# Moving the C-row multiply of 49 scan steps from VectorE to GpSimd

## The chip, the cores and the metric

The kernel runs on one core of one Trainium2 chip. The metric is the device time of one execution in microseconds.

## What is computed

Two layers act on x of shape (4, 1024, 128) in fp32. Layer 0 adds to x the product of a Mamba block (a selective scan with 256 inner channels and 16 states) and a gated mixture of experts (8 experts, 2 chosen per token, and a shared one). Layer 1 does the same with an attention without softmax, and a second mixture of experts. The part that the change touches is the selective scan:

```python
dA = jnp.exp(dt[..., None] * A)
dBx = (dt * xc)[..., None] * Bm[:, :, None, :]
def step(h, inp):
    dA_t, dBx_t, C_t = inp
    h = dA_t * h + dBx_t
    y = jnp.einsum('bdn,bn->bd', h, C_t)
    return (h, y)
_, ys = lax.scan(step, h0, (dA, dBx, Cm))        # over time
y = (ys + xc * D_param) * silu(z)
```

## The kernel before, in words

Time is cut into eight chunks of 512, of which the last is two segments of 256. In each of the nine segments there are 16 scan steps, one for each state n, so there are 144 steps, N = 0 to 143; steps 0 to 111 are wide (512 columns in each of two halves of the channels) and 112 to 143 narrow (256). Channels lie on the partitions, time along the free axis. A segment that starts in the middle of a batch entry needs, for each state, the last column of the segment before it; that column is kept in `carry` by steps 0 to 15, 32 to 47, 64 to 79 and 96 to 127.

One step N is shared by the engines:

- ACT computes exp(dt * A) into `pA` in PSUM (line 1016, function `decay`, for step N+1 while step N is scanned). It waits for the product of step N, since `pA` is one buffer, and for the carried column, which ACT itself copies (line 1162). It then issues the DMA that loads the B and C rows of step N+3, spread over all partitions, into `bcb` (line 1025, `bc_load`), which waits until step N has let go of that buffer.
- GpSimd multiplies dt*x by the B row into `dBx` (line 805), for step N+1 as soon as the first scan of step N is over.
- VectorE does two scans in place in `pA` (line 1429) and then multiplies `pA` by the C row into `hc` in SBUF (line 1437). `hc` has two buffers; the multiply waits until the transposes of step N-2 have read the one it writes.
- TensorE transposes `hc` (line 902, `hflip`, eight transposes in a wide step, four in a narrow one) and sums the states in the PSUM tensor `pH`.

Beside the scan every step carries other work, and its order is written out by `make_plan`; all engines walk the same list and each does its own part of every item. A step is "a scan b hflip", or "a scan b c hflip" when a second job starts. The slots a, b and c are pipelined expert jobs: `gate` is two VectorE operations (lines 1465 and 1477, each with one operand in PSUM), `up` two matmuls of TensorE with a tanh on ACT (lines 1181, 1186), and `flip` transposes and the down matmuls, read back by ACT (lines 1196, 1199). Slots a and c are of lane 0, b of lane 1. Behind `hflip` come the step's extras: parts of the mixer's front (conv, line 1377; subtraction, line 1402; softplus and others), normalisation (line 1243), routing (lines 1293 to 1363), the combination of expert outputs (partly on GpSimd, lines 774 and 778), and scatters and gathers, which GpSimd issues as indirect DMAs. Many of VectorE's extras are linked: each waits for a semaphore of the one before.

Of the kernel before, what the change touches and what calls it, by code (L numbers as in the profile page):

```python
# [11 lines left out]
P = 128  # L12
# [5 lines left out]
NS = 16  # L18
# [59 lines left out]
def make_plan():  # L78
# [175 lines left out]
    plan += [("decay", 0)]  # L254
    running, waiting = [None, None], [None, None]
# [26 lines left out]
    for step in range(max(end + 3, max(extras) + 1)):  # L282
# [8 lines left out]
        for what in order:  # L291
# [4 lines left out]
            elif what == "scan":  # L296
                if ends_chunk:
                    plan.append(("accT", q - 1))
                if live:
                    plan.append(("scan", step))  # L300
            elif what in ("a", "b", "c"):
                new = starts.get((step, 0), {}).get("ab".find(what)) if what != "c" else starts[step, 1][0]
                before_slot = len(plan)
                slot(1 if what == "b" else 0, new, step)
                if what.upper() in order and (what == "b" or running[0] is None or lanes[0][running[0]][0] == 1) and len(plan) > before_slot and plan[-1][0] == "flip":
                    held.append((what, plan.pop()))
# [5 lines left out]
            elif what == "hflip":  # L312
                if ends_chunk:
                    plan.append(("y", q - 1))
                if live:
                    plan.append(("hflip", step))
                if ends_chunk:
                    plan.append(("mix_out", q - 1))
# [9 lines left out]
def program(nc, T, out):  # L328
# [29 lines left out]
    for N in range(STEPS):  # L358
        s, n = divmod(N, NS)
        if s + 1 < len(SEGS) and SEGS[s + 1][0] // 2 == SEGS[s][0] // 2:  # L360
            carry_no[N] = len(carry_no) + 1
            carry_after[N + NS] = carry_no[N]

# [11 lines left out]
    with ExitStack() as ctx:  # L375
# [188 lines left out]
        zs_ready, acc_copied = sem("zs_ready"), sem("acc_copied")  # L564
        mixed_stored, gathered, fetched, combined, mid_stored, out_stored = (
# [150 lines left out]
        def _(pool):  # L716
            for kind, *a in plan:
# [75 lines left out]
                elif kind in ("decay", "scan"):  # L793
# [11 lines left out]
                    pool.tensor_tensor(dBx[:, N % 2, :, 0:t1 - t0], dtx[q % 2][:, :, t0:t1], row, ALU.mult).then_inc(dBx_ready, 1)  # L805


        @block.tensor
        def _(pe):
# [12 lines left out]
            for kind, *a in plan:  # L822
# [68 lines left out]
                elif kind == "hflip":  # L891
# [3 lines left out]
                    pe.wait_ge(hc_ready, N + 1)  # L895
# [9 lines left out]
                elif kind == "busy":  # L905
                    pe.wait_ge(hc_ready, STEPS)
# [95 lines left out]
        def _(act):  # L1002
            A = act.activation

            def decay(N):
# [5 lines left out]
                if N:  # L1011
                    act.wait_ge(hc_ready, N)
                    if N - 1 in carry_no:
                        act.wait_ge(carried, carry_no[N - 1])
# [3 lines left out]
            def bc_load(N):  # L1018
# [3 lines left out]
                if N >= BCR:  # L1022
                    act.wait_ge(dBx_ready, N - BCR + 1)
                    act.wait_ge(hc_ready, N - BCR + 1)
                act.dma_start(*bc_row(N)).then_inc(bc_loaded[N % BCR], 16)

            for kind, *a in plan:
# [129 lines left out]
                elif kind == "scan":  # L1157
                    N, = a
                    q, t0, t1 = SEGS[N // NS]
                    if N in carry_no:  # L1160
                        act.wait_ge(hc_ready, N + 1)
# [57 lines left out]
        def _(dve):  # L1219
# [28 lines left out]
            for kind, *a in plan:  # L1248
# [172 lines left out]
                elif kind == "scan":  # L1421
# [3 lines left out]
                    if N in carry_after:  # L1425
                        dve.wait_ge(carried, carry_after[N])
                    for k in range(DK):
                        dve.wait_ge(decay_ready, 2 * N + k + 1)
                        dve.tensor_tensor_scan(pA[:, k, 0:w], pA[:, k, 0:w], dBx[:, N % 2, k, 0:w],  # L1429
                                               carry[:, k, N % NS:N % NS + 1] if N in carry_after else 0.0, ALU.mult, ALU.add  # L1430
                                               ).then_inc(h_ready, 1)

                    dve.wait_ge(h_ready, 2 * N + 2)
# [157 lines left out]
```

## Time and profile before

| what | value |
|---|---|
| time, median of 3 runs | 1128.32 us (1124.17 to 1129.85) |
| profiled execution, first to last instruction (the profile gives no other time of it) | 1123.9 us |
| VectorE busy | 960.6 us, 85% |
| TensorE busy | 895.5 us, 80% |
| GpSimd busy | 613.3 us, 55% |
| ACT busy | 607.2 us, 54% |

The profile names the engines PE (TensorE matmul), PEld (its weight load), DVE (VectorE), ACT, POOL (GpSimd) and SP. Busy time is the union of an engine's recorded instructions. A line such as L1437 is line 1437 of the kernel before. "a<-b,c" gives the written tensor and the ones read; idle time stands with what ended it.

### The profile page before, as it was taken

Reading aid. Unit: us, or ns where it says so; the run is one execution under the profiler, and the core shown is the slowest. Engines: PE = TensorE matmul, PEld = TensorE weight load, DVE = VectorE, ACT = ScalarE, POOL = GpSimd, SP = SyncE. Lnnn points to the kernel's source line nnn. Section 1 sums busy time; section 2 is a strip of 40 time slices with the busy share of each in tenths; the row PEclk is TensorE's granted clock in tenths of the full one; section 3 lists DMA queues with packets and bytes.
Section 4 is the critical chain, followed back from the end, with each engine's and each line's share of the span. In section 5 each row is a group of like instructions: output and inputs, shape, how many; then the busy total and the mean of one; then the engine's idle time right before and its main releaser. Section 6 shows DMA issues by size and latency. Waiting matters only on the chain.

```text
span 1123.9 us, 16984 instructions
## 1 busy us (share of the span) xinstructions
PE 895.5 (80%) x4556; PEld 633.1 (56%) x4556; DVE 960.6 (85%) x1804; ACT 607.2 (54%) x1593; POOL 613.3 (55%) x422
## 2 busy tenths in 40 slices
PE   3466688778787778897997799898876888889878
PEld 1344466556565555675665466665555656556556
DVE  4698878999999998998999899999969878978445
ACT  2444556574456564665666466665554555546243
POOL 1238423768634846675327855665874747425540
PEclk9986789997898898999999899999977999989999
DMA  9955344356543644565444645455742466446201
GB/s 277 298 128 133 85 101 110 119 133 180 118 101 106 141 102 117 148 164 146 111 96 127 156 129 150 102 162 145 192 111 73 109 155 159 109 102 142 73 9 34
DMA packets 168650, 144.71 MB, mean 129 GB/s; under 512 B 15680, under 2 KB 135536, under 8 KB 168560
## 3 DMA queue, kind: packets, MB, share of 16 engines
q10 hardware_dynamic: 39776, 67.47, 27.5%
q1 hardware_dynamic: 121104, 60.43, 18.9%
q0 software_dynamic: 7680, 15.74, 4.6%
q8 instruction: 41, 0.67, 0.2%
q14 instruction: 49, 0.40, 0.1%
HBM read 106.88 MB, written 36.70 MB: 128 GB/s over the span
## 4 chain that ended last, share of the span: by engine, by line
DVE 37%; PE 32%; issue 15%; ACT 8%; DMA 4%; POOL 3%; ACTq 1%; DVEq 0%; SPq 0%; another core or an unknown queue 0%; POOLq 0%
DVE pA L1429 14%; PE pM L996 5%; PE pH L902 5%; DVE hj L1465 4%; PE pM L986 3%; PE p L961 3%; DVE ca L1377 2%; PE pG L958 2%; DVE hj L1477 2%; DVE hc L1437 2%; PE pH L974 2%; DMA bcb<-bc_rows 2%; PE pU L959 2%; POOL dBx L805 1%; PE pG L961 1%
## 5 line engine op out<-in xcount | busy, mean ns | idle before, releaser
L805 POOL TENSOR_TENSOR dBx<-dtx,bcb 128x1024 f32<-128x1024 f32 (+1 forms) x144 | 304.6, 2116 | 364.7 <-DVE pA L1429 339.0
L902 PE MATMUL pH<-const,hc 128*128 128x128 f32 x1024 | 161.8, 305 | 42.3 <-DVE hc L1437 38.8
L1016 ACT ACTIVATE pA<-dt,am 128x512 f32<-128x512 f32 (+1 forms) x288 | 173.9, 639 | 17.2 <-DVE hc L1437 9.5
L1429 DVE TENSOR_TENSOR_SCAN pA<-pA,carry,dBx 128x512 f32<-128x512 f32 (+1 forms) x160 | 162.8, 1063 | 19.5 <-ACT pA L1016 14.4
L902 PEld LDWEIGHTS pH<-const,hc 128*128 128x128 f32 x1024 | 129.0, 157 | 62.9 <-DVE hc L1437 47.1
L1437 DVE TENSOR_TENSOR hc<-pA,bcb 128x1024 f32<-128x1024 f32 (+1 forms) x144 | 159.3, 1106 | 5.0
L1429 DVE TENSOR_TENSOR_SCAN pA<-pA,dBx 128x512 f32<-128x512 f32 x128 | 149.8, 1215 | 13.8 <-ACT pA L1016 8.8
L986 PE MATMUL pM<-const,hj 128*128 128x128 f32 (+3 forms) x636 | 127.7, 297 | 34.2 <-DVE hj L1477 14.2
L747 POOL DMA_INDIRECT rows_in<-xn,slots x120 | 131.6, 1096 | 30.3 <-issue 29.1
L1196 ACT ACTIVATE yj<-pM 128x128 f32<-128x128 f32 x236 | 65.5, 277 | 129.9 <-PE pM L996 119.8
L986 PEld LDWEIGHTS pM<-const,hj 128*128 128x128 f32 (+3 forms) x636 | 71.4, 138 | 107.9 <-issue 75.2
L1199 ACT ACTIVATE hT<-pM 128x256 f32<-128x256 f32 (+1 forms) x272 | 113.7, 418 | 26.6 <-PE pM L986 25.1
L958 PE MATMUL pG<-w13a,xgT 128*128 x184 | 83.0, 535 | 43.2 <-DVE hj L1477 40.0
L763 POOL DMA_INDIRECT gy<-rows_out,slots x96 | 98.4, 1025 | 24.6 <-issue 21.0
L996 PE MATMUL pM<-w2b,hT 128*128 (+1 forms) x448 | 97.2, 318 | 1.6 <-ACT hT L1199 0.9
L1465 DVE SCALAR_TENSOR_TENSOR hj<-tj,pG 128x352 f32<-128x352 f32 (+2 forms) x153 | 68.2, 446 | 22.3 <-ACT tj L1181 9.2
L996 PEld LDWEIGHTS pM<-w2b,hT 128*128 128x128 f32 x448 | 71.8, 201 | 21.5 <-issue 5.7
L996 PE MATMUL pM<-w2a,hT 128*128 x552 | 80.7, 284 | 0.0
L959 PE MATMUL pU<-w13a,xgT 128*128 x184 | 77.3, 505 | 0.0
L996 PEld LDWEIGHTS pM<-w2a,hT 128*128 128x128 f32 x552 | 73.6, 203 | 0.1
L961 PE MATMUL p<-w13b,xgT 128*128 x106 | 49.4, 551 | 28.9 <-DVE hj L1477 18.6
L958 PEld LDWEIGHTS pG<-w13a,xgT 128*128 128x128 f32 x184 | 30.8, 203 | 69.8 <-issue 69.1
(208 smaller groups left out, 1530.9 us busy)
## 6 DMA issues: line engine op xcount, KB each, us to landing
bcb<-bc_rows ACTq DMA_DIRECT2D x112, 512.0 KB
rows_out<-yj SPq DMA_DIRECT2D x236, 64.0 KB
xg<-rows_in SPq DMA_DIRECT2D x176, 64.0 KB
bcb<-bc_rows ACTq DMA_DIRECT2D x32, 256.0 KB
rows_in<-gy SPq DMA_DIRECT2D x8, 512.0 KB, 8.9
mixed<-s_st SPq DMA_DIRECT2D x12, 256.0 KB
so<-rows_out SPq DMA_DIRECT2D x6, 512.0 KB
sr<-mixed SPq DMA_DIRECT2D x6, 512.0 KB
```

Source lines behind the costliest of these rows:

```text
L747: pool.indirect_dma_start(rows_in[l][b % 2], bass.IndirectOffsetOnAxis(ap=slots[l][b][:, c, k:k + 1], axis=0), xn[:, c, :], None).then_inc ...
L805: pool.tensor_tensor(dBx[:, N % 2, :, 0:t1 - t0], dtx[q % 2][:, :, t0:t1], row, ALU.mult).then_inc(dBx_ready, 1)
L902: last = mm(pH[:, half, c * DI + k * P:c * DI + (k + 1) * P], hc[:, N % 2, k, t * P:(t + 1) * P], ident, is_transpose=True, start=(n == 0 ...
L958: mm(pG[:, 0:hid], tok, w[:, 0:hid], start=True, stop=True).then_inc(gate_full, 1)
L959: mm(pU[:, 0:hid], tok, w[:, hid:2 * hid], start=True, stop=True).then_inc(gu_full[i], 1)
L986: last = pe.transpose(pM[0:w, m * P:(m + 1) * P], hj[i][:, k % 2, m * P:m * P + w], ident)
L996: last = mm(pM[:, YA:YA + P], hT[i][0:wd, m * P:(m + 1) * P], w[0:wd, m, :], start=(m == 0), stop=(m == len(ks) - 1))
L1016: A(pA[:, k, 0:t1 - t0], dt[q % 2][:, k, t0:t1], ACT.Exp, scale=am[:, k, n:n + 1]).then_inc(decay_ready, 1)
L1199: last = A(hT[i][:, 0:w], pM[:, 0:w], ACT.Copy)
L1429: dve.tensor_tensor_scan(pA[:, k, 0:w], pA[:, k, 0:w], dBx[:, N % 2, k, 0:w], carry[:, k, N % NS:N % NS + 1] if N in carry_after else 0.0, ...
L1437: dve.tensor_tensor(hc[:, N % 2, :, 0:w], pA[:, :, 0:w], row, ALU.mult).then_inc(hc_ready, 1)
L1465: dve.scalar_tensor_tensor(out=hj[i][:, k % 2, 0:hid], in0=tj_of(i, k), scalar=1.0, in1=gate_bank(i, k)[:, 0:hid], op0=ALU.add, op1=ALU.mu ...
```

## The change

`make_plan` finds the steps in which GpSimd has no scatter, gather, normalisation power or combination to do, and leaves out the last step of each segment. These "quiet" steps are 0-4, 11-14, 16-20, 27, 28, 38-43, 51-53, 67, 69-75, 88, 98, 109, 115-117, 128 and 130-138: 36 wide and 13 narrow ones. In them

- the scans write `hc` in SBUF instead of `pA`, and so wait for the transposes of step N-2 before they start;
- the multiply by C is done by GpSimd in place in `hc`, as a plan item `weigh` behind `scan`, thus behind GpSimd's `dBx` of step N+1; in the steps whose last column is carried GpSimd copies it first, and waits for that copy;
- `decay` of step N+1 waits for the scans alone, and `bc_load` of step N+3 for GpSimd's product;
- `hflip` stands behind slot a of step N+1.

```diff
+    busy_pool = {step for step, items in extras.items() for it in items
+                 if it[0] in ("scatter", "gather", "norm") or it[0] == "combine" and on_pool(*it[1:3]) and 0 <= it[3] < 3}
+    quiet = {N for N in range(STEPS) if N not in busy_pool and N % NS != NS - 1}
...
                     plan.append(("scan", step))
+                    if step in quiet:
+                        plan.append(("weigh", step))
...
                 slot(1 if what == "b" else 0, new, step)
+                if what == "a" and step - 1 in quiet:
+                    plan.append(("hflip", step - 1))
...
-                if live:
+                if live and step not in quiet:
                     plan.append(("hflip", step))
...
+        def product_done(N):
+            return (hc_ready_pool if N in on_gpsimd else hc_ready), weighed[N]
...
+                elif kind == "weigh":
+                    N, = a
+                    w = SEGS[N // NS][2] - SEGS[N // NS][1]
+                    pool.wait_ge(h_ready, 2 * N + 2)
+                    if N in carry_no:
+                        pool.tensor_copy(carry[:, :, N % NS], hc[:, N % 2, :, w - 1]).then_inc(carried_pool, 1)
+                        pool.wait_ge(carried_pool, carries_pool[N])
+                    row = bcb[:, N % BCR, 1:2, 0:w].broadcast_to([P, DK, w])
+                    pool.tensor_tensor(hc[:, N % 2, :, 0:w], hc[:, N % 2, :, 0:w], row, ALU.mult).then_inc(hc_ready_pool, 1)
...
-                    pe.wait_ge(hc_ready, N + 1)
+                    pe.wait_ge(*product_done(N))
...
                 if N:
-                    act.wait_ge(hc_ready, N)
-                    if N - 1 in carry_no:
-                        act.wait_ge(carried, carry_no[N - 1])
+                    if N - 1 in on_gpsimd:
+                        act.wait_ge(h_ready, 2 * N)
+                    else:
+                        act.wait_ge(*product_done(N - 1))
+                        if N - 1 in carry_no:
+                            act.wait_ge(*carry_done(N - 1))
...
                 if N >= BCR:
                     act.wait_ge(dBx_ready, N - BCR + 1)
-                    act.wait_ge(hc_ready, N - BCR + 1)
+                    act.wait_ge(*product_done(N - BCR))
...
-                    if N in carry_no:
-                        act.wait_ge(hc_ready, N + 1)
+                    if N in carry_no and N not in on_gpsimd:
+                        act.wait_ge(*product_done(N))
...
+                    if N in on_gpsimd and N >= 2:
+                        dve.wait_ge(hflip_full, N - 1)
                     for k in range(DK):
                         dve.wait_ge(decay_ready, 2 * N + k + 1)
-                        dve.tensor_tensor_scan(pA[:, k, 0:w], pA[:, k, 0:w], dBx[:, N % 2, k, 0:w],
+                        h = hc[:, N % 2, k, 0:w] if N in on_gpsimd else pA[:, k, 0:w]
+                        dve.tensor_tensor_scan(h, pA[:, k, 0:w], dBx[:, N % 2, k, 0:w],
                                                carry[:, k, N % NS:N % NS + 1] if N in carry_after else 0.0, ALU.mult, ALU.add
                                                ).then_inc(h_ready, 1)
+                    if N in on_gpsimd:
+                        continue
```

## Rows read from the trace of the kernel before

**Rows 1.** The page, part 1: engine, busy us, share of the span, instructions.

```profile
PE 895.5 (80%) x4556; PEld 633.1 (56%) x4556; DVE 960.6 (85%) x1804; ACT 607.2 (54%) x1593; POOL 613.3 (55%) x422
```

**Rows 2.** The page, part 4: the chain that ended last, share by engine.

```profile
DVE 37%; PE 32%; issue 15%; ACT 8%; DMA 4%; POOL 3%; ACTq 1%; DVEq 0%; SPq 0%; another core or an unknown queue 0%; POOLq 0%
```

**Rows 3.** Windows A:B, length, busy PE, PEld, DVE, ACT, POOL; clock; DMA. All steps; 38-43; 136.

```profile
43.88:1044.70 1000.82, 815.06 (x4218) 584.05 (x4218) 904.67 (x1653) 565.30 (x1494) 582.76 (x390) 0.91 0.52 130
312.89:353.46 40.57, 34.63 (x178) 25.70 (x178) 39.38 (x83) 23.78 (x57) 14.16 (x6) 0.87 0.38 95
1012.55:1016.56 4.01, 4.01 (x25) 2.92 (x24) 3.28 (x7) 2.76 (x11) 1.27 (x1) 1.00 0.48 113
```

**Rows 4.** VectorE by form: busy us, mean ns, idle before. Scans and the C multiply.

```profile
L1429 DVE TENSOR_TENSOR_SCAN pA<-pA,dBx 128x512 f32<-128x512 f32 x128 | 149.8, 1215 | 13.8 <-ACT pA L1016 8.8 <-POOL dBx L805 5.0
L1429 DVE TENSOR_TENSOR_SCAN pA<-pA,carry,dBx 128x512 f32<-128x512 f32 x96 | 118.1, 1276 | 10.0 <-ACT pA L1016 9.3 <-POOL dBx L805 0.6
L1437 DVE TENSOR_TENSOR hc<-pA,bcb 128x1024 f32<-128x1024 f32 x112 | 137.1, 1224 | 3.8
L1437 DVE TENSOR_TENSOR hc<-pA,bcb 128x512 f32<-128x512 f32 x32 | 22.1, 692 | 1.1
```

**Rows 5.** One line each, GpSimd: duration ns min/median/max, first and last start.

```profile
L805 POOL TENSOR_TENSOR dBx<-dtx,bcb x144: 1257/2352/2386, 41.5 to 1041.2; 128x1024 f32<-128x1024 f32 x112, 128x512 f32<-128x512 f32 x32
L778 POOL TENSOR_TENSOR gy<-gy x5: 2347/2362/2808, 307.8 to 1074.9; 128x1024 f32<-128x1024 f32 x5
```

**Rows 6.** Timeline of step 53: start us, duration us, engine, line.

```profile
416.51 2.46 DVE L1429 TENSOR_TENSOR_SCAN pA<-pA,carry,dBx 128x512 f32<-128x512 f32 x2
419.00 1.22 DVE L1437 TENSOR_TENSOR hc<-pA,bcb 128x1024 f32<-128x1024 f32 x1
420.14 2.32 DVE L1377 SCALAR_TENSOR_TENSOR ca<-xs,cw,ca 128x512 f32<-128x512 f32 x3
417.94 2.35 POOL L805 TENSOR_TENSOR dBx<-dtx,bcb 128x1024 f32<-128x1024 f32 x1 [4.82 <-DVE pA L1429]
```

**Rows 7.** VectorE's conv line (min/median/max); timeline at 307 and at 289.

```profile
L1377 DVE SCALAR_TENSOR_TENSOR ca<-xs,cw,ca x48: 741/752/2905, 15.0 to 788.6; 128x512 f32<-128x512 f32 x48
307.67 4.32 DVE L1377 SCALAR_TENSOR_TENSOR ca<-xs,cw,ca 128x512 f32<-128x512 f32 x3
307.84 2.81 POOL L778 TENSOR_TENSOR gy<-gy 128x1024 f32<-128x1024 f32 x1
289.94 3.42 DVE L1243 TENSOR_SCALAR xn<-x,mv,rstd 128x128 f32<-128x128 f32 x3
288.54 2.37 POOL L805 TENSOR_TENSOR dBx<-dtx,bcb 128x1024 f32<-128x1024 f32 x1
290.85 1.91 POOL L774 TENSOR_TENSOR gy<-gy,wts 128x1024 f32<-128x1024 f32 x1
```

**Rows 8.** Timeline of step 43.

```profile
345.85 2.34 DVE L1429 TENSOR_TENSOR_SCAN pA<-pA,dBx 128x512 f32<-128x512 f32 x2
349.36 0.76 DVE L1402 TENSOR_SCALAR xs<-ca 128x1024 f32<-128x1024 f32 x1
350.15 0.23 DVE L1346 TENSOR_TENSOR over<-rk,const 128x64 f32<-128x64 f32 x1
347.21 2.36 POOL L805 TENSOR_TENSOR dBx<-dtx,bcb 128x1024 f32<-128x1024 f32 x1 [4.74 <-DVE pA L1429]
```

**Rows 9.** Timeline: first held operation of step 4 and of step 109.

```profile
74.12 2.32 DVE L1377 SCALAR_TENSOR_TENSOR ca<-xs,cw,ca 128x512 f32<-128x512 f32 x3
860.30 0.22 DVE L1346 TENSOR_TENSOR over<-rk,const 128x64 f32<-128x64 f32 x1
```

**Rows 10.** Timeline of step 40: its scans, and ACT's tanh for the second job.

```profile
324.72 2.34 DVE L1429 TENSOR_TENSOR_SCAN pA<-pA,dBx 128x512 f32<-128x512 f32 x2
330.33 0.46 ACT L1181 ACTIVATE tj<-pG 128x352 f32<-128x352 f32 x1 [0.41 <-PE pG L958]
```

**Rows 11.** The page, part 5: the transposes into pH.

```profile
L902 PE MATMUL pH<-const,hc 128*128 128x128 f32 x1024 | 161.8, 305 | 42.3 <-DVE hc L1437 38.8
```

More of the change, by code:

```diff
@@ L362, in program @@
             carry_after[N + NS] = carry_no[N]
+    on_gpsimd = {it[1] for it in plan if it[0] == "weigh"}
+    weighed = {N: sum(m <= N for m in on_gpsimd) if N in on_gpsimd else sum(m not in on_gpsimd for m in range(N + 1))
+               for N in range(STEPS)}
     routed_before = {i: [sum(j[2] == "routed" for j in lanes[i][:k]) for k in range(len(lanes[i]) + 1)] for i in lanes}
@@ L564, in program, with carry_done @@
         zs_ready, acc_copied = sem("zs_ready"), sem("acc_copied")
+        hc_ready_pool, carried_pool = sem("hc_ready_pool"), sem("carried_pool")
+        def product_done(N):
+            return (hc_ready_pool if N in on_gpsimd else hc_ready), weighed[N]
+        carries_pool = {N: n + 1 for n, N in enumerate(m for m in sorted(carry_no) if m in on_gpsimd)}
+        carries_act = {N: n + 1 for n, N in enumerate(m for m in sorted(carry_no) if m not in on_gpsimd)}
+        def carry_done(N):
+            return (carried_pool, carries_pool[N]) if N in on_gpsimd else (carried, carries_act[N])
         mixed_stored, gathered, fetched, combined, mid_stored, out_stored = (
@@ L905, in _ @@
                 elif kind == "busy":
[L906 removed]
+                    pe.wait_ge(*product_done(STEPS - 1))
                     for c in range(a[0]):
@@ L1425, in _ @@
                     if N in carry_after:
-                        dve.wait_ge(carried, carry_after[N])
+                        dve.wait_ge(*carry_done(N - NS))
+                    if N in on_gpsimd and N >= 2:
+                        dve.wait_ge(hflip_full, N - 1)
                     for k in range(DK):
                         dve.wait_ge(decay_ready, 2 * N + k + 1)
-                        dve.tensor_tensor_scan(pA[:, k, 0:w], pA[:, k, 0:w], dBx[:, N % 2, k, 0:w],
+                        h = hc[:, N % 2, k, 0:w] if N in on_gpsimd else pA[:, k, 0:w]
+                        dve.tensor_tensor_scan(h, pA[:, k, 0:w], dBx[:, N % 2, k, 0:w],
                                                carry[:, k, N % NS:N % NS + 1] if N in carry_after else 0.0, ALU.mult, ALU.add
                                                ).then_inc(h_ready, 1)
+                    if N in on_gpsimd:
+                        continue
                     dve.wait_ge(h_ready, 2 * N + 2)
```

## The prediction

> **What bounds the kernel now.** I read the totals of the page first. VectorE is busy for 85% of the span and TensorE for 80% [rows 1]. The chain of waits gives 37% to VectorE and 32% to TensorE [rows 2], so the two alternate and neither alone is the bound. Cut to the 144 scan steps (1000.8 us, 6.95 us each on average), VectorE is busy 904.7 us, TensorE 815.1 and GpSimd only 582.8 [rows 3]. The first row of that group says that GpSimd has time to give; the others say where VectorE's time would be worth something. In steps 38 to 43, six of the 49 that the change calls quiet, VectorE is busy 39.4 of 40.6 us: each microsecond on VectorE there is a microsecond of the kernel. In step 136, as in 135, 137 and 138 beside it, TensorE is busy 4.01 of 4.01 us and VectorE 3.28: there VectorE's time is worth nothing. I went through all 49 steps in the timeline in this way.
>
> **What is taken away.** The multiply by the C row leaves VectorE in the quiet steps: 36 wide ones (chunks of 512) at 1.224 us and 13 narrow ones (256) at 0.692 us [rows 4], 44.1 + 9.0 = 53.1 us of VectorE work. The scans stay at 1.215 us each [rows 4]; that they write SBUF instead of PSUM I cost at nothing, since the multiply itself goes from PSUM to SBUF and its 1024 columns take what the page shows for any such pass. No row shows a scan of that width into SBUF: 0.06 us a scan either way, the spread between the scan without and with a carried start, would be 98 x 0.06 = 6 us either way.
>
> **What GpSimd gets.** A multiply of two SBUF operands over 1024 columns. The nearest rows are its own dBx multiply, median 2.352 us, 1.257 at its shortest (narrow), and an add in place, 2.362 at the median and 2.808 at most [rows 5]; a multiply by a per-token weight took 1.91 [rows 7]. I take 2.35 wide and 1.27 narrow, bounds 1.9 and 2.8. By the plan it stands behind dBx of the next step. In a wide step dBx(N+1) starts 1.4 us after the scans start and ends at +3.75 [rows 6, 8], so the new multiply runs from +3.75 to +6.1. The next dBx is wanted at about +8, so GpSimd keeps up with its own work. In 28 of the 49 steps it also copies the carried column; no row shows such a copy on GpSimd, and I take 0.2 us (between 0, hidden, and the multiply's own 2.35, the nearest row however far).
>
> **What that does to VectorE.** This term decides. The operations of VectorE that read two SBUF operands do not run while GpSimd computes. The conv line, whose three operations are otherwise 0.75 us each, has a longest one of 2.905 us [rows 7]. The pair of rows at 307 shows the mechanism: GpSimd's add is issued at 307.84, while the first of three linked conv operations runs, takes 2.81 instead of 2.36 us, and the three conv operations take 4.32 us together instead of 2.32 [rows 6, 7]. So a GpSimd operation that waits takes the gap between two linked VectorE operations, and VectorE then waits it out. The three rows at 289 show that it is worse when two GpSimd operations stand back to back: VectorE's first normalise operation is issued at 289.94, before dBx ends at 290.91, and yet waits over the following GpSimd multiply too (to 292.76); the first three of them, 128 columns each, stand with 3.42 us, where a pass of 512 columns takes 0.74. In the kernel before, GpSimd is silent from +3.75 on in quiet steps, and the multiply by C (one operand in PSUM, 1.224 us with dBx beside it) fills VectorE until then: the two do not collide. The change moves VectorE's further work up to +2.4, under dBx, and puts 2.35 us of GpSimd behind it.
>
> Step 53 (no carry) [rows 6]: scans until 418.97, dBx until 420.29, three conv operations from 420.14. Afterwards the first conv operation is ready at 419.0, is held by dBx and then by the new multiply, 420.3 to 422.65, and starts at about 422.45 (both cases of rows 7 let VectorE go on 0.2 before GpSimd's record ends). That is 2.3 us later than now. Step 43 (carry) [rows 8]: the subtraction on VectorE gets in between the carried copy and the multiply, the multiply then runs from about 350.4 to 352.7, and the comparison that starts at 350.15 now starts at about 352.5: 2.35 later. In both the 1.22 us gained are eaten by what is left of dBx, and a full GpSimd multiply is lost.
>
> Step by step, with the place of the first held operation now (behind the scans' start) against the multiply's end at +5.9 to +6.5:
> - Two-operand work right behind the scans, more than one linked operation (or no carry): steps 11, 27, 39, 41, 42, 43, 51, 53, 67, 71, 75, 11 x 2.35 = 25.9 us.
> - Such work behind one pair of gate operations, or later: 4 (0.9), 17 (1.8), 18 (1.3), 20 (0.8), 28 (1.6), 40 (1.2), 52 (1.6), 69, 73, 74, 109 (1.9 each), 98 (1.2), sum 18.0 us. Of the 23 wide steps of both lists the first and the last are in [rows 9]: in step 4 the conv operations start at +4.8 and the second one slips, in 109 the comparison starts at +4.1.
> - Narrow steps with such work: 115, 130, 133, 134, sum 2 us.
> - The other 22: no such work (3, 13, 14, 19, 117, 135 to 138), one operation only, or work that now comes after +6. There the multiply's place is either returned to TensorE or gained for a few tenths; I count 1.5 us gained in all.
> VectorE therefore ends 25.9 + 18.0 + 2 - 1.5 = 44 us later in sum.
>
> How much of that reaches the end: in steps 38 to 43 all of it at first, since VectorE idles 1.2 of 40.6 us. But over all scan steps VectorE idles 96 us [rows 3], mostly in steps that TensorE fills, and TensorE catches up while VectorE is late. I take 30% as absorbed, a choice between nothing (97% busy in steps 38 to 43) and 60% (the idle time that steps like 136 have, 18%, would cover most of a lateness within two or three of them, but few such steps stand near). 44 x 0.7 = 31 us.
>
> **The rest of the change.** ACT's exponentials may start after the scans instead of after the multiply, and lose 28 carried copies. But ACT then issues the load of a later B/C row, which now waits for GpSimd's product. Behind it on ACT are the tanh and the copies of the second job, of the stage work and of the next step's first slot. In step 40 the scans start at 324.72 and the second job's tanh at 330.33 [rows 10]; afterwards ACT is released at 324.72 + 6.3 = 331.0 and the tanh is 0.7 us late. It costs nothing, because VectorE is by then held longer; without that cover it costs up to 0.7 us in a step with a second job, some 10 us over 15 such steps. The row itself has two steps to land, so its DMA is not late. The transposes (161.8 us in all, 1.1 us a step) [rows 11] come behind the next gate, up and flip. They wait for a product at +6.1 to +7.4, which is before TensorE has done that slot, and they take the place where TensorE waited for the gate of the second job: a few tenths gained, up to their 38.8 us of recorded waits, mostly off the path. I take 0. The scans' wait for the transposes of two steps before comes 2.4 us earlier than now and is met.
>
> **The rivals.**
> - First come, first served: a VectorE operation that has waited through dBx runs before the multiply also where no carried copy lies between. Then steps 17 and 27 lose nothing (4.15 us less) and 18 a little less: 5 us of the 44, and 1123.9 + 39 x 0.7 = 1151 for the profiled run, 1155.5 for the median. For it: in every carry step I count on such a gap. Against: the operation issued at 289.94 stood before the second GpSimd multiply and did not run first [rows 7].
>   "SBUF — State Buffer", section "Who interferes with whom", of the Trainium skill has this order: a VectorE instruction with two SBUF inputs contends with a GpSimd one that reads SBUF, and whichever issues first holds the shared ports for its whole length. By that page alone the time would be the one of this rival; the trace agrees on the lock and not, in the one case at 289.94, on the order.
> - VectorE is served first, and keeps the port between linked operations. If its waiting operation, and the next linked one, win the port over the new multiply, only dBx's remainder costs. Each step of the first list is a wash, each of the second gains about 0.7 us, 12 x 0.7 + 3 = 11, times 0.7 is 8: 1120 us (1116 to 1127). For it: nothing but the small gaps (0.03 us) between linked operations. Against: both cases of rows 7.
> - The gain as meant, the other side of the forecast: VectorE sheds 53.1 us and nothing is held. Some 34 steps bound by VectorE, 38 us of the 53, times 0.7: 27 us, 1101 us. It decides from the point at which GpSimd's multiply no longer overlaps two-operand work; the timeline puts such work in 36 or more of the 49 steps, so it is unlikely.
> - Nothing is absorbed, and ACT's wait adds its 10: 44 + 10 = 54, 1182 us. For it: VectorE at 97% in steps 38 to 43.
>
> **How the numbers follow.** The profiled execution spans 1123.9 us, which becomes 1155; the median of the runs shown is 1128.3, 4.4 above that span, and becomes 1159. Chances: forecast 0.62, first come 0.10, the worse case 0.07, VectorE first 0.13, the full gain 0.08. A difference under 0.5% (5.6 us) can hardly be told from none. Slower 0.62 + 0.10 + 0.07 = 0.79; of the 0.13 I give 0.05 to faster and 0.08 to no change, so faster is 0.13. The likeliest case's own range is 1138 to 1175; the range given, 1124 to 1180, takes in part of the second case.
>
> **What would show it.** In the profile after: 49 GpSimd multiplies of 2.35 or 1.27 us; conv, normalise, combine and routing operations on VectorE with longest durations near 3 to 4 us and means up (the conv line from 0.854 to over 1.2); VectorE's busy time nearly as high as before in spite of 53 us less work; quiet steps 1 to 2.5 us longer where listed and 135 to 138 unchanged. The prediction is wrong if those operations keep their durations while the new multiplies run beside them, or if steps 41, 43 and 53 shorten.

## The result, and the profile after

The changed kernel takes 1159.91 us in the median of four runs (1159.24 to 1162.34), against 1128.61 for the kernel before on the same chip: ratio 1.0286, 95% interval [1.0248, 1.0323]. It is 2.9% slower. The profiled execution spans 1160.5 us, 36.6 more than before. One execution each of e6 (2687 us) and e10 (1619 us) and one of the kernel before (1197 us) lie far from all others and are in none of the ratios below.

The busy line and the chain by engine of the page after (they answer to [rows 1, 2]):

```profile
PE 920.7 (79%) x4556; PEld 654.0 (56%) x4556; DVE 969.5 (84%) x1755; ACT 602.0 (52%) x1565; POOL 733.8 (63%) x499
DVE 35%; PE 30%; POOL 12%; issue 12%; ACT 6%; DMA 4%; ACTq 1%; DVEq 0%; POOLq 0%; SPq 0%
```

VectorE has lost 53 us of multiplies and is nonetheless busy for 8.9 us more (969.5 against 960.6). GpSimd's share of the chain has gone from 3% to 12%. VectorE by form (busy us, mean ns, idle before):

```profile
L1479 DVE TENSOR_TENSOR hc<-pA,bcb 128x1024 f32<-128x1024 f32 x76 | 93.1, 1225 | 2.6
L1469 DVE TENSOR_TENSOR_SCAN hc<-pA,dBx 128x512 f32<-128x512 f32 x50 | 58.3, 1208 | 11.4 <-ACT pA L1053 8.1 <-POOL dBx L829 3.2
L1414 DVE SCALAR_TENSOR_TENSOR ca<-xs,cw,ca 128x512 f32<-128x512 f32 x48 | 50.2, 1046 | 7.5 <-ACT ca L1137 6.3
L1280 DVE TENSOR_SCALAR xn<-x,mv,rstd 128x128 f32<-128x128 f32 x40 | 20.7, 582 | 2.7 <-POOL rstd L758 2.7
L1439 DVE TENSOR_SCALAR xs<-ca 128x1024 f32<-128x1024 f32 x8 | 11.9, 1494 | 9.7 <-ACT ca L1175 9.7
L1386 DVE TENSOR_TENSOR_SCAN incl<-const,nt 128x8 f32<-128x8 f32 x8 | 7.0, 873 | 0.3
L1359 DVE TENSOR_TENSOR picked<-oh 128x64 f32<-128x64 f32 x7 | 6.0, 854 | 0.2
L1340 DVE TENSOR_TENSOR pr<-el,se 128x64 f32<-128x64 f32 x7 | 5.7, 817 | 0.2
```

The scans that write SBUF take 1.208 us, no more than those in PSUM (1.215, [rows 4]). The C multiply has 76 and 19 instances left of 112 and 32. The conv line went from 41.0 us to 50.2, mean from 0.854 to 1.046; the subtraction, L1439, from 5.8 to 11.9; and operations on 8 or 64 columns (L1386, L1359, L1340) now average 0.8 to 0.9 us where they averaged 0.17, 0.27 and 0.22. GpSimd's new lines, of the same view:

```profile
L839 POOL TENSOR_TENSOR hc<-hc,bcb 128x1024 f32<-128x1024 f32 x36 | 91.1, 2532 | 2.0
L839 POOL TENSOR_TENSOR hc<-hc,bcb 128x512 f32<-128x512 f32 x13 | 17.5, 1345 | 0.2
L836 POOL COPY carry<-hc 128x2 f32<-128x2 f32 x28 | 14.0, 500 | 0.0
```

Without the C multiply VectorE was busy for 960.6 - 137.1 - 22.1 = 801.4 us before and is for 969.5 - 93.1 - 13.1 = 863.3 us now. No operation was added to it, so its operations are 61.9 us longer: that is what it is held. Not all of them are: the gate of 352 columns, which reads one operand from PSUM, takes 0.515 us as before, the C multiply from PSUM 1.225 (1.224), and a reduction of 64 columns of SBUF (L1385) 0.220 (0.220), though many of them run beside GpSimd's work (in step 43 the reduction lies at 365.71, under the multiply). The subtraction L1439, which is stretched, reads only one tensor and adds a constant, so it is not the second operand alone that makes an operation wait. 61.9 - 53.1 is the 8.9 us net. The other 27.7 us of the span are idle time of VectorE (163.3 before, 191.0 now), and part of it stands before the gates, which wait for a tanh of ACT: this line stood with 12.5 us idle, 9.2 of it for ACT, and now has

```profile
L1507 DVE SCALAR_TENSOR_TENSOR hj<-tj,pG 128x352 f32<-128x352 f32 x92 | 47.4, 515 | 20.1 <-ACT tj L1218 19.1 <-DVE idx L1345 0.3
```

ACT in turn waits for GpSimd's product, at the row load, before whatever comes next on it. These are the five largest of twelve such lines (us in total, times, longest); all twelve are 58 us:

```profile
ACT tj L1223 <- POOL hc L839: 10.2, 4, 4.9
ACT zs L1187 <- POOL hc L839: 7.2, 3, 3.3
ACT tj L1218 <- POOL hc L839: 7.0, 4, 2.4
ACT xgT L1211 <- POOL hc L839: 6.7, 4, 2.2
ACT lg L1081 <- POOL hc L839: 5.2, 1, 5.2
```

How VectorE is held shows in the steps. Step 53 after, to be laid beside [rows 6] (start, duration):

```profile
437.00 2.45 DVE L1469 TENSOR_TENSOR_SCAN hc<-pA,carry,dBx 128x512 f32<-128x512 f32 x2
439.37 5.50 DVE L1414 SCALAR_TENSOR_TENSOR ca<-xs,cw,ca 128x512 f32<-128x512 f32 x3
445.44 1.28 DVE L1469 TENSOR_TENSOR_SCAN pA<-pA,carry,dBx 128x512 f32<-128x512 f32 x1
438.42 2.36 POOL L829 TENSOR_TENSOR dBx<-dtx,bcb 128x1024 f32<-128x1024 f32 x1 [3.33 <-DVE hc L1469]
440.75 2.78 POOL L839 TENSOR_TENSOR hc<-hc,bcb 128x1024 f32<-128x1024 f32 x1
```

The first conv operation is issued at 439.37, under dBx; the three take 5.50 us where they took 2.32, and the step 8.44 instead of 6.52. One by one they are recorded from 439.37 to 441.33, 441.37 to 444.08 and 444.12 to 444.87. GpSimd's multiply is recorded with 2.78 us from 440.75, so it waited as well: VectorE's first conv operation ran between dBx and the multiply, the second one after it. Step 27, with one such operation:

```profile
244.53 1.96 DVE L1439 TENSOR_SCALAR xs<-ca 128x1024 f32<-128x1024 f32 x1
243.60 2.34 POOL L829 TENSOR_TENSOR dBx<-dtx,bcb 128x1024 f32<-128x1024 f32 x1 [1.32 <-DVE hc L1469]
245.90 2.79 POOL L839 TENSOR_TENSOR hc<-hc,bcb 128x1024 f32<-128x1024 f32 x1
```

It waits for dBx alone (1.96 us instead of 0.70), GpSimd's multiply waits for it, and the step is as long as before (5.02 us, 5.04 before). Step 43, with a carried column, to be laid beside [rows 8]:

```profile
363.40 2.02 DVE L1439 TENSOR_SCALAR xs<-ca 128x1024 f32<-128x1024 f32 x1
365.97 1.95 DVE L1386 TENSOR_TENSOR_SCAN incl<-const,nt 128x8 f32<-128x8 f32 x1
362.51 2.36 POOL L829 TENSOR_TENSOR dBx<-dtx,bcb 128x1024 f32<-128x1024 f32 x1 [0.18 <-DVE hc L1469]
364.81 0.66 POOL L836 COPY carry<-hc 128x2 f32<-128x2 f32 x1
365.55 2.34 POOL L839 TENSOR_TENSOR hc<-hc,bcb 128x1024 f32<-128x1024 f32 x1
```

The subtraction is held by dBx, the carried copy by the subtraction (0.66 us), and then the multiply starts beside a VectorE operation and holds an 8-column scan for 1.95 us instead of 0.17. The step takes 9.38 us instead of 7.61.

The same can be summed over all steps, each from its first scan to the first scan of the next. The 11 steps of the prediction's first list are 19.6 us longer than before, about 12.5 of it VectorE's busy time and 7.0 its idle time. The 12 of the second list are 13.4 us longer, 5.8 busy and 7.6 idle. The other 26 quiet steps are 1.1 us longer: VectorE is busy for 10.2 us less there and idle for 11.3 more. The steps that were not changed add 1.1 us.

### The profile page after: what moved, and what is told of

It reads as the page before. It is cut to its first block, busy times and chain, and to the rows that moved or that the text cites. A ratio compares the mean times of both kernels' runs of the same rounds, so it can differ in the third digit from the quotient of the medians.

```text
span 1160.5 us, 16934 instructions
## 1 busy us (share of the span) xinstructions
PE 920.7 (79%) x4556; PEld 654.0 (56%) x4556; DVE 969.5 (84%) x1755; ACT 602.0 (52%) x1565; POOL 733.8 (63%) x499
## 4 chain that ended last, share of the span: by engine, by line
DVE 35%; PE 30%; POOL 12%; issue 12%; ACT 6%; DMA 4%; ACTq 1%; DVEq 0%; POOLq 0%; SPq 0%
DVE pA L1469 9%; POOL dBx L829 6%; PE pM L1030 4%; DVE hj L1507 4%; PE pM L1020 3%; DVE hc L1469 3%; PE pH L936 3%; POOL hc L839 3%; PE pG L992 3%; DVE ca L1414 3%; PE p L995 3%; PE pU L993 2%; POOL gy L787 2%; PE pH L1008 2%; DVE xn L1280 2%
## 5 line engine op out<-in xcount | busy, mean ns | idle before, releaser
L1020 PE MATMUL pM<-const,hj 128*128 128x128 f32 (+3 forms) x636 | 131.0, 303 | 34.3 <-DVE hj L1519 13.9
L936 PEld LDWEIGHTS pH<-const,hc 128*128 128x128 f32 x1024 | 132.4, 159 | 37.0 <-DVE hc L1479 20.8
L1469 DVE TENSOR_TENSOR_SCAN pA<-pA,carry,dBx 128x512 f32<-128x512 f32 (+1 forms) x112 | 117.6, 1095 | 12.5 <-ACT pA L1053 9.5
L992 PE MATMUL pG<-w13a,xgT 128*128 x184 | 86.7, 558 | 36.4 <-DVE hj L1519 35.9
L839 POOL TENSOR_TENSOR hc<-hc,bcb 128x1024 f32<-128x1024 f32 (+1 forms) x49 | 108.6, 2217 | 2.2
L1479 DVE TENSOR_TENSOR hc<-pA,bcb 128x1024 f32<-128x1024 f32 (+1 forms) x95 | 106.2, 1118 | 3.3
L1469 DVE TENSOR_TENSOR_SCAN pA<-pA,dBx 128x512 f32<-128x512 f32 x78 | 91.3, 1215 | 5.2 <-ACT pA L1053 4.5
L1030 PE MATMUL pM<-w2a,hT 128*128 x552 | 84.0, 292 | 0.0
L993 PE MATMUL pU<-w13a,xgT 128*128 x184 | 80.1, 521 | 0.0
L1030 PEld LDWEIGHTS pM<-w2a,hT 128*128 128x128 f32 x552 | 76.6, 209 | 0.2
L992 PEld LDWEIGHTS pG<-w13a,xgT 128*128 128x128 f32 x184 | 32.9, 215 | 63.0 <-issue 62.3
```

The costliest lines, as they stand in the source:

```text
L839: pool.tensor_tensor(hc[:, N % 2, :, 0:w], hc[:, N % 2, :, 0:w], row, ALU.mult).then_inc(hc_ready_pool, 1)
L936: last = mm(pH[:, half, c * DI + k * P:c * DI + (k + 1) * P], hc[:, N % 2, k, t * P:(t + 1) * P], ident, is_transpose=True, start=(n == 0 ...
L992: mm(pG[:, 0:hid], tok, w[:, 0:hid], start=True, stop=True).then_inc(gate_full, 1)
L1020: last = pe.transpose(pM[0:w, m * P:(m + 1) * P], hj[i][:, k % 2, m * P:m * P + w], ident)
L1030: last = mm(pM[:, YA:YA + P], hT[i][0:wd, m * P:(m + 1) * P], w[0:wd, m, :], start=(m == 0), stop=(m == len(ks) - 1))
L1469: dve.tensor_tensor_scan(h, pA[:, k, 0:w], dBx[:, N % 2, k, 0:w], carry[:, k, N % NS:N % NS + 1] if N in carry_after else 0.0, ALU.mult, A ...
```

## The experiments

Each ran beside the kernel before on the same chip; there it took 1127.8, 1130.7 or 1131.6 us in the median. So runs are compared by their ratio, and where the text gives a difference in us it is the ratio less 1, times 1128. The expectations name absolute times. The last columns are VectorE's busy time in the profiled run less 960.6 us, and its idle time in the span (163.3 us before). e1, e6 and e3 leave out products with C, so they are no candidates. The profile of e3 is that of its longest execution, 1141.2 us against a median of 1128.9; that of e13 is its longest too (1145.3, median 1140.6), that of e11 its shortest (1135.5, median 1142.1).

| run | ratio to before (95%) | VectorE's busy time | its idle time |
|---|---|---|---|
| the change | 1.0286 [1.0248, 1.0323] | +8.9 | 191.0 |
| e1_write_only | 1.0106 [1.0063, 1.0150] | -22.8 | 197.9 |
| e2_late_load | 1.0269 [1.0226, 1.0312] | +22.6 | 174.3 |
| e6_late_load_write_only | 0.9916 [0.9879, 0.9954] | -8.2 | 167.4 |
| e3_half | 0.9981 [0.9947, 1.0016] | -12.9 | 190.8 |
| e5_added_mult | 1.0270 [1.0227, 1.0313] | +36.6 | 159.9 |
| e9_held_steps | 1.0131 [1.0092, 1.0170] | +14.4 | 164.5 |
| e13_second_list | 1.0085 [1.0060, 1.0109] | +7.3 | 174.7 |
| e8_clean_late | 1.0018 [0.9985, 1.0052] | -10.7 | 181.5 |
| e4_flips_back | 1.0369 [1.0322, 1.0415] | +4.0 | 202.4 |
| e10_under_scans | 1.0059 [1.0022, 1.0096] | +6.2 | 170.7 |
| e11_split_late | 1.0104 [1.0063, 1.0145] | +12.2 | 160.9 |
| e12_under_some | 1.0039 [1.0018, 1.0060] | +1.1 | 171.9 |

**e5_added_mult: the hold alone.** On the kernel before:

```diff
+                elif kind == "weigh":
...
+                    pool.wait_ge(h_ready, 2 * N + 2)
+                    same = dtx[q % 2][:, :, t0:t1]
+                    pool.tensor_tensor(dBx[:, N % 2, :, 0:t1 - t0], same, same, ALU.mult).then_inc(junk_done, 1)
```

The item stands behind `scan` in the same 49 steps. Only GpSimd itself waits for it, before a later dBx goes into the same buffer.

> The kernel before, with one thing added: in the same 49 steps GpSimd squares dt*x into the free dBx buffer, behind its dBx work, 2.35 or 1.27 us; nobody waits for it and VectorE keeps its multiply by C. If GpSimd's reads hold VectorE's two-operand operations, those behind the multiply (from +3.7 us in a wide step) are held by up to 2.35 us each step: 40-60 us of stretched operations and a time of 1150-1175 us. If GpSimd's work is harmless to VectorE, 1126-1131 us.

Measured 1157.39 us, ratio 1.0270. Its busy line and its conv line:

```profile
PE 910.1 (79%) x4556; PEld 643.6 (56%) x4556; DVE 997.2 (86%) x1804; ACT 610.1 (53%) x1593; POOL 698.3 (60%) x471
L1392 DVE SCALAR_TENSOR_TENSOR ca<-xs,cw,ca 128x512 f32<-128x512 f32 x48 | 45.2, 942 | 7.4 <-ACT ca L1115 6.3
```

VectorE issues what it did before and is busy 36.6 us longer; the conv line's mean went from 0.854 to 0.942. Its idle time did not rise (159.9 us against 163.3), so no new wait is behind it. The time rises by 2.7%, 30 us, so that 80% of the hold arrives at the end. A GpSimd operation that no other engine waits for costs as much as the whole change. This shows the hold and its price; the size of 40 to 60 us was too high.

**e1_write_only: no reads.** On the changed kernel:

```diff
-                    pool.tensor_tensor(hc[:, N % 2, :, 0:w], hc[:, N % 2, :, 0:w], row, ALU.mult).then_inc(hc_ready_pool, 1)
+                    pool.memset(hc[:, N % 2, :, 0:w], 0.0).then_inc(filled, 1)
+                    pool.wait_ge(filled, 2 * weighed[N] - 1)
+                    pool.memset(hc[:, N % 2, :, 0:w], 0.0).then_inc(filled, 1)
+                    pool.wait_ge(filled, 2 * weighed[N])
+                    pool.memset(hc[:, N % 2, 0, 0:w // 2], 0.0).then_inc(hc_ready_pool, 1)
```

> The changed kernel, but GpSimd's multiply in the 49 steps is replaced by three fills of the same buffer (1024, 1024 and 512 columns in a wide step, about 2.4 us together), so GpSimd is as long at work and everybody waits for it as before, but it reads nothing from SBUF. The product with C is left out there. If what costs is that GpSimd's reads hold VectorE's two-operand operations, the held time of the new multiply goes, the conv line's mean is back near 0.85 us, VectorE's busy time falls from 969.5 to about 910 us and the time from 1160 to 1105-1125 us. If the cost lies in the waits for GpSimd's product (ACT's row load, the transposes), the time stays at 1150-1162 us.

Measured 1139.34 us, ratio 1.0106, between the two expectations and in neither. Three lines of it, to be laid beside those of the change:

```profile
L1418 DVE SCALAR_TENSOR_TENSOR ca<-xs,cw,ca 128x512 f32<-128x512 f32 x48 | 43.5, 907 | 7.5 <-ACT ca L1141 6.3
L1363 DVE TENSOR_TENSOR picked<-oh 128x64 f32<-128x64 f32 x7 | 1.9, 276 | 0.2
L1443 DVE TENSOR_SCALAR xs<-ca 128x1024 f32<-128x1024 f32 x8 | 13.0, 1628 | 8.1 <-ACT ca L1179 8.1
```

The conv line is most of the way back to 0.854 and one 64-column product is back at 0.27 us (the other, `pr`, only from 0.82 to 0.63), but the subtraction is stretched as much as in the change. VectorE's busy time fell as expected in direction, by 31.7 us against the change (937.8; I had said about 910: dBx still holds what now starts under it, and one-operand subtractions and normalisations are held too), but the kernel is slower than before with 22.8 us less of busy time on VectorE. Step 71 of this run shows on what:

```profile
558.91 0.28 ACT L1237 ACTIVATE yj<-pM 128x128 f32<-128x128 f32 x1 [1.42 <-POOL hc L843]
561.71 0.22 ACT L1085 ACTIVATE lg<-pM 128x64 f32<-128x64 f32 x1 [2.25 <-PE pM L880]
559.51 2.16 PE L880 MATMUL pM<-gate,xnT 128*128 128x8 f32 x16 [2.02 <-ACT hT L1240]
557.01 2.34 DVE L1473 TENSOR_TENSOR_SCAN hc<-pA,dBx 128x512 f32<-128x512 f32 x2
561.97 0.22 DVE L1334 TENSOR_REDUCE mx<-lg 128x8 f32<-128x64 f32 x1 [2.62 <-ACT lg L1085]
```

ACT's read-back waits 1.42 us for GpSimd's last fill, TensorE's logits 2.0 us for ACT, ACT for the logits, and VectorE stands for 2.6 us before it can take the maximum. That is the rival named in the expectation, and it is real once VectorE is held less.

**e2_late_load and e6_late_load_write_only: ACT's wait.** The same edit on the change and on e1:

```diff
-                    if N + BCR < STEPS:
+                    if N + BCR < STEPS and N not in on_gpsimd:
                         bc_load(N + BCR)
+                elif kind == "hflip" and a[0] in on_gpsimd and a[0] + BCR < STEPS:
+                    bc_load(a[0] + BCR)
```

> The changed kernel, but in the 49 steps ACT issues the row load not right behind the exponentials but where the transposes now stand, behind slot a of the next step, so that nothing on ACT waits for GpSimd's product early. By the prediction's sum that wait was covered and costs nothing: 1155-1160 us. If ACT's wait is a cost of its own (VectorE's idle time rose by 28 us between the two traces, mostly before operations that wait for a tanh), the time falls to 1135-1148 us.

> The two edits of e1_write_only (1139.3 us) and e2_late_load (1157.3 us) together: GpSimd fills the buffer instead of multiplying by C (the product is left out in the 49 steps), and ACT's row load stands behind slot a of the next step. In the trace of e1 ACT's read-back waits up to 1.7 us a step for GpSimd, TensorE's logits for ACT and VectorE for the logits. If the wait on ACT is a cost that only VectorE's held operations cover, it shows once they are gone: 1118-1130 us. If what is left in e1 is VectorE held by dBx alone, the late load brings as little as in e2: 1135-1141 us.

Measured 1157.34 us (1.0269) and 1121.58 us (0.9916). The busy lines, of e1, e2 and e6:

```profile
PE 901.7 (79%) x4556; PEld 641.0 (56%) x4556; DVE 937.8 (83%) x1755; ACT 601.7 (53%) x1565; POOL 723.7 (64%) x597
```

```profile
PE 909.2 (79%) x4556; PEld 646.9 (56%) x4556; DVE 983.2 (85%) x1755; ACT 607.2 (52%) x1565; POOL 740.2 (64%) x499
```

```profile
PE 878.1 (78%) x4556; PEld 622.9 (56%) x4556; DVE 952.4 (85%) x1755; ACT 606.3 (54%) x1565; POOL 725.0 (65%) x597
```

With the reads in place the late load moves the ratio by 0.0017, inside the intervals. Without them it moves it by 0.0190, 21 us. Seen the other way, taking the reads away is worth 0.018 (20 us) with ACT's wait in place and 0.035 (40 us) without it. The two costs cover each other. How they do it is only in part shown. In e2, with ACT free, VectorE is busy for 14 us more than in the change (983.2 against 969.5) and idle for 17 less; in the 23 steps of the two lists together nothing changes (32.9 us longer than before, 33.0 in the change), 7.6 us of idle time having become busy time. But in e6 VectorE is also busy for 14.6 us more than in e1, and there its idle time falls by 30.5 us. So the extra hold alone does not tell the two cases apart, and why the idle time falls less with the reads in place is not shown.

**e3_half: half the reads.**

```diff
-                    row = bcb[:, N % BCR, 1:2, 0:w].broadcast_to([P, DK, w])
-                    pool.tensor_tensor(hc[:, N % 2, :, 0:w], hc[:, N % 2, :, 0:w], row, ALU.mult).then_inc(hc_ready_pool, 1)
+                    row = bcb[:, N % BCR, 1:2, 0:w].broadcast_to([P, 1, w])
+                    pool.tensor_tensor(hc[:, N % 2, 0:1, 0:w], hc[:, N % 2, 0:1, 0:w], row, ALU.mult).then_inc(hc_ready_pool, 1)
```

> The changed kernel, but GpSimd multiplies only the first of the two channel halves in the 49 steps (512 or 256 columns, about 1.25 or 0.7 us; the product of the other half with C is left out). If VectorE is held for as long as GpSimd reads, the held time falls by up to half of what the multiply added, and the time lies midway between 1160 and the 1139 of the fill: 1144-1151 us. If each GpSimd operation costs by being there, whatever its length, 1155-1160 us.

Measured 1128.94 us, ratio 0.9981. Halving 2.35 us of GpSimd work in 49 steps gives back the whole loss, 3.1%. I had expected half of it, so this is a miss. It shortens both costs at once: in its profile ACT waits 33 us for GpSimd's product instead of 58, and VectorE is busy for 22 us less than in the change. That two costs that cover each other have to go together fits this, and is not shown by this run alone. VectorE sheds its 53 us there, and still nothing is gained.

**e9_held_steps and e13_second_list: which steps.** `quiet` cut to the 11 steps of the prediction's first list, and to the 12 of its second, one line in each kernel:

```diff
+    quiet &= {11, 27, 39, 41, 42, 43, 51, 53, 67, 71, 75}
...
+    quiet &= {4, 17, 18, 20, 28, 40, 52, 69, 73, 74, 98, 109}
```

> The changed kernel with the change in only 11 of the 49 steps, those of the prediction's first list (11, 27, 39, 41, 42, 43, 51, 53, 67, 71, 75), where two-operand work of VectorE follows the scans at once. The prediction's sum gives 11 x 2.35 = 25.9 us on VectorE and 18 us at the end: 1144-1149 us. If the loss is spread over the 49 steps by some other cause (a lower TensorE clock, GpSimd's load), 11 of them carry 11/49 of 31 us: 1134-1137 us.

> The change in only the 12 steps of the prediction's second list (4, 17, 18, 20, 28, 40, 52, 69, 73, 74, 98, 109), where two-operand work stands behind a pair of gates or later. The prediction gives 18.0 us on VectorE, 12.6 at the end: 1139-1143 us. With e9's 11 steps at +14.8 us and the whole change at +31.6, a rest of 15 to 17 us for these and the other steps is what addition leaves: 1140-1145. If VectorE gets in ahead of the multiply, as in step 53 of the changed kernel, and nothing else costs: 1130-1136 us.

Measured 1.0131 (14.8 us for the first list, by the sum 18) and 1.0085 (9.6 us for the second, by the sum 12.6). In absolute times e9, 1141.01 us, lies between its two expectations, and e13, 1140.58, inside the first two of its three. Together they are 24.4 of the 32 us. The rest, 8 us with an interval of some 7 either way, is small: in the trace of the change the two lists are longer by 19.6 and 13.4 us and all other quiet steps by 1.1, where the first list is longer by 13.3 us in the trace of e9 and the second by 12.5 in that of e13. So it is the first list's steps that grow more when all are changed, and not the other steps. 11 steps carry nearly half of the loss, where 11/49 would be 7 us: it is tied to where such work stands, not spread.

**e8_clean_late: the other steps.** `quiet` cut to 16 steps without such work right behind the scans, with the late load of e2.

```diff
+    quiet &= {13, 14, 16, 19, 70, 72, 88, 116, 117, 128, 131, 134, 135, 136, 137, 138}
```

> The change in only 16 of the 49 steps (13, 14, 16, 19, 70, 72, 88, 116, 117, 128, 131, 134 to 138), those in which no two-operand work of VectorE, or one operation or late work only, follows the scans, and with the late row load. If two-operand work under GpSimd is what costs, these steps are neutral or gain: 1121-1131 us. If moving the multiply and the transposes costs by itself, 16/49 of 31 us: 1136-1140 us.

Measured 1134.33 us, in neither expectation, but by its ratio of 1.0018 [0.9985, 1.0052] no change, and less than the 10 us of the second. VectorE sheds 10.7 us net and idles for 18 more. In the trace before, TensorE is busy for 91% of these 16 steps and VectorE for 85%; in the steps of the first list it is 77% and 98%, in those of the second 80% and 94%. So where VectorE's time would be worth most, work follows that is held.

**e4_flips_back: the transposes.** `hflip` at the end of its own step, as before.

```diff
-                if what == "a" and step - 1 in quiet:
-                    plan.append(("hflip", step - 1))
...
-                if live and step not in quiet:
+                if live:
```

> The changed kernel with the transposes of the 49 steps back at the end of their own step, where they wait for GpSimd's product on TensorE. The prediction put the place of the transposes at 0: 1156-1163 us, if TensorE's wait is covered by what holds VectorE. If their place matters, TensorE stands before the product until +6 to +7.4 us of a step, with the stage work's matmuls and the next slot behind it: 1166-1185 us.

Measured 1170.20 us, ratio 1.0369 against 1.0286, some 9 us more, on intervals that just touch. TensorE's waits for the product show it (us in total, times, longest):

```profile
PEld pH L934 <- POOL hc L837: 69.9, 21, 18.5
PE pH L934 <- POOL hc L837: 65.0, 21, 18.1
```

In the change these two waits for GpSimd's product are 1.7 and 0.4 us; before, the waits for VectorE's product were 47.1 and 38.8 us in all 144 steps. So the time fell into my other expectation, near its lower end: the new place of the transposes is worth some 9 us against the old one. The prediction's 0 compared it with the kernel before, and no run shows that difference.

**Versions meant to be better.** e10 puts GpSimd's multiply under the scans of the next step:

```diff
                 if live:
+                    if step - 1 in quiet:
+                        plan.append(("weigh", step - 1))
                     plan.append(("scan", step))
-                    if step in quiet:
-                        plan.append(("weigh", step))
+                    if step - 1 in quiet:
+                        plan.append(("hflip", step - 1))
...
                     pool.wait_ge(h_ready, 2 * N + 2)
+                    gates = [it[2] for it in plan[:plan.index(("weigh", N))] if it[:2] == ("gate", 0)]
+                    if gates:
+                        pool.wait_ge(hj_ready[0], gates[-1] + 1)
```

`gates[-1]` is the last gate of lane 0 planned ahead of the multiply, so that GpSimd doesn't start it under that gate. The `hflip` behind slot a is gone, and ACT issues the row load at the new `weigh`. e12 is e10 with

```diff
+    quiet &= {2, 4, 18, 20, 28, 40, 52, 70, 72, 74, 88, 98, 109, 116, 128, 131}
```

> A version meant to be better, with all 49 steps: GpSimd's multiply of step N is put off until VectorE has done the gate of slot a in step N+1, so that it runs under that step's scans, which have one SBUF operand; dBx of step N+2 follows it, 1 us later than now; the transposes and the row load follow too. If only two-operand work beside GpSimd's reads costs, the multiply is free, but what stands right behind the scans meets the later dBx: 1118-1138 us, well under 1160. If the cost is GpSimd's extra 109 us of work wherever it stands, or the wait chain, 1150-1170 us.

> As e10_under_scans, but in 16 steps only (2, 4, 18, 20, 28, 40, 52, 70, 72, 74, 88, 98, 109, 116, 128, 131), those in which VectorE has gates or other one-operand work right behind the scans, so that what it sheds is not eaten by the rest of dBx. By the theory VectorE sheds 18 us there and is held little more than before: 1115-1126 us. If GpSimd's later dBx and the moved transposes cost as much as is shed: 1127-1135 us.

> A version meant to be better: in the 49 steps VectorE multiplies the first channel half by C from PSUM (0.66 us) and GpSimd only the second, in place (about 1.25 us), and the row load stands behind slot a of the next step. VectorE sheds 24 us instead of 53, is held by half-length multiplies, and ACT's wait is gone. From the time of e3_half, in which VectorE multiplied neither half (ratio 0.998), plus about 24 us of VectorE's work, less some 5 to 15 us for the late load: 1125-1140 us. If the multiply's length is all that matters it falls below 1120 us.

e10 measured 1.0059, with all 49 steps and all of GpSimd's work: 2.3% better than the change, and still no gain. Its dBx ends 5.1 us after the scans start in the median of the wide steps that follow a changed one, where it ended at 3.7, and VectorE is held about as long as in the change (busy without C for 860.6 us, 863.3 in the change). What it has gained on the change is idle time, 170.7 us instead of 191.0. e12, 16 steps of it, measured 1.0039, a miss: I had expected a gain. e11, GpSimd with one channel half and VectorE with the other,

```diff
+                        dve.tensor_tensor(hc[:, N % 2, 0, 0:w], pA[:, 0, 0:w], bcb[:, N % BCR, 1, 0:w], ALU.mult).then_inc(half_ready, 1)
```

measured 1142.05 us, ratio 1.0104, a miss as well. No version that computes everything beats the kernel before; e6 and e3 are at or below its time only by leaving out products with C.

## Why the prediction came out right, and which of its steps did not

**Right: the direction and the places.** The listed steps are the ones that grew, by 19.6 and 13.4 us, where the prediction's sum times 0.7 gives 18.1 and 12.6.

**Right with luck: the size.** 1159 us forecast, 1159.9 measured, but VectorE's net work grew by 8.9 us and not by 44, and a wait that the sum put at nothing made up for it.

**Right: the cause.** VectorE's operations with two SBUF operands do not run beside GpSimd's multiply. It rested on three rows of the trace before [rows 7]; e5 shows it by addition, e1 by removal of the reads. The section "Who interferes with whom" of "SBUF — State Buffer" of the Trainium skill states it, and the traces agree (0.27 us with fills, 0.85 with the multiply, for the 64-column product). The prediction's wording is too narrow: its own cases at 289.94 and in steps 27 and 43 are a normalisation and a subtraction of one tensor, and both are stretched. And it was one of two causes, not the only one.

**Wrong: the order of two GpSimd operations back to back.** From 289.94 I took it that VectorE waits over both. In steps 27 and 53 it ran between them. In the whole trace after, 19 VectorE operations are issued under one GpSimd operation with another right behind it and are stretched by over 0.2 us; 18 of them ran first, 12 before a carried copy and 5 before the new multiply, and one did not, the same normalisation as at 289.94. So the rival "first come, first served", which is the order that the same section of the Trainium skill states, describes the steps after. That at 289 stays unexplained. Where a GpSimd operation is issued while a VectorE operation runs, it goes before the next linked one, as in steps 43 and 53 and at 307.

**Wrong in size: "VectorE therefore ends 44 us later in sum".** That was 97 us of hold less 53 shed. Measured are 61.9 of hold, 8.9 net; with ACT free (e2) 75.7 and 22.6. Steps 27 and 42, each counted at 2.35, lost nothing.

**Wrong: "it costs nothing" for ACT's wait.** Taking it away is worth 2 us with the reads in place (e2) and 21 without them (e6 against e1). Yet it is not free in the change: 16.7 of the 27.7 us of new idle time are gone in e2, replaced by hold. The total came out because the two errors offset each other, 35 us too much hold against a wait priced at nothing.

**Not borne out: the 30% absorbed.** 36.6 us of hold became 30 in e5, and 14.4 net became 14.8 in e9, in which ACT waits 18 us for GpSimd. In the runs where ACT waits for GpSimd's product at most 2 us, VectorE's net work and the time are: e2 +22.6 and +30, e5 +36.6 and +30, e6 -8.2 and -9, e11 +12.2 and +12, e10 +6.2 and +7, e12 +1.1 and +4, e8 -10.7 and +2. They go together within 8 us, except in e8, in most of whose steps TensorE has more to do than VectorE; no one share for what is absorbed comes out of them.

**Smaller points.** Steps 41, 43 and 53 grew by 1.8 to 2.0 us, steps 136 to 138 did not change, 135 grew by 1.2. The scan into SBUF costs nothing, as taken. GpSimd's carried copy takes 0.19 us in the median, as taken, and up to 1.58 us when held. TensorE's granted clock was 0.884 in the profiled run against 0.916, and TensorE was busy for 25.2 us more. But nine runs of the kernel before at 0.887 to 0.911 took 1122 to 1133 us without an order in it, and on the two other chips 0.01 less clock went with some 1.5 us more time, loosely. The four runs of the change had 0.884 to 0.902, so at most a few us of the 31 can be the clock's.

**Open.** Where the 11 us of idle time come from that are left when ACT's wait is taken away (e2), why the late load brings so much less with the reads in place, and why the first list's steps grow more in company (19.6 us in the trace of the change) than alone (13.3 us in that of e9).

## What to carry to other kernels

Before work is moved from VectorE to GpSimd, list the VectorE operations that will stand beside it and look in a trace which of them are stretched beside GpSimd's work. Here those with two SBUF operands were, and subtractions, normalisations and casts of one; reductions and operations with an operand in PSUM were not. An idle GpSimd is no free engine if it shuts out work that then stands on the path. Look also at each queue that gets a wait on the slower engine's product, here a DMA issue in the middle of ACT's work. Two such costs can cover each other, so that taking away either alone shows little; remove both before judging one.

## What the runs showed of the hardware that was not expected

- GpSimd is held as VectorE is: its multiply of 1024 columns takes 2.35 us in the median and up to 3.34, a copy of two columns 0.19 and up to 1.58.
- GpSimd's fills, which read nothing, still hold VectorE's subtraction of one SBUF operand: its eight instances took 13.0 us in e1, 5.8 before. In step 27 of e1 it waits over dBx and the first fill and is over at 241.53, 0.55 us after that fill; the second fill then takes 1.38 us instead of 0.95:

```profile
238.68 2.85 DVE L1443 TENSOR_SCALAR xs<-ca 128x1024 f32<-128x1024 f32 x1
240.04 0.94 POOL L839 MEMSET hc<- 128x1024 f32 x1
241.04 1.38 POOL L841 MEMSET hc<- 128x1024 f32 x1
```

- So the same subtraction that ran before the new multiply in the change (1.96 us) is passed over by the fill in e1 (2.85 us). Of eight stretched operations that stood before the first fill in e1, three were passed over, a subtraction, a normalisation and a cast; the four with two SBUF operands and one more normalisation ran first. In the trace before (289.94) and in that after (299.05) it happened once, to a normalisation and with a GpSimd multiply. What decides it is open.
